# First-stage pieces, degree operations and clearing in other slots of a four-layer graph kernel

## The reference

```python
x = layernorm(x + L0(x, adj))            # prelu(adj @ (x @ W) + bias)
x = layernorm(x + L1(x, adj))            # adj @ (x @ weight) + bias
x = layernorm(x + L2(x, adj, nodemask))  # 5 rounds of message passing with a gated cell:
    # A = (adj != 0); m = h @ weight[l]; agg = A.T @ m
    # r, z = sigmoid(...); n = tanh(i_n + r * h_n); h = (1 - z) * n + z * h
x = layernorm(x + L3(x, adj, ...))       # 5 groups of the first 25 nodes: two graph convolutions each,
    # norm_adj = dinv * (adj + I) * dinv, dinv = deg ** -0.5, mixed with softmax(fusion_w)
```

## Time and profile before

| | us |
|---|---|
| median of 3 runs | 990.35 (988.59 to 992.75) |
| profiled execution | 988.7 |
| its span, first to last instruction | 986.9 |
| PE busy | 950.6 (96%) |
| DVE busy | 820.8 (83%) |
| ACT busy | 770.9 (78%) |
| POOL busy | 749.0 (76%) |

### The profile page before, as it was taken

How to read it: one execution, slowest core, us unless ns; L and a number is a source line. 1 busy time by engine, 2 the same in 40 slices (tenths; PEclk the granted TensorE clock), 3 DMA queues, 4 the chain that set the end, 5 groups by cost and what they waited for, 6 DMA issues and landing times.

```text
span 986.9 us, 19418 instructions
## 1 busy us (share of the span) xinstructions
PE 950.6 (96%) x6010; PEld 574.5 (58%) x6010; DVE 820.8 (83%) x2077; ACT 770.9 (78%) x1324; POOL 749.0 (76%) x844
## 2 busy tenths in 40 slices
PE   7999998999999999999999999999999999989894
PEld 6999996554444544444554555554445455468783
DVE  5999998898879999988898899789879987946555
ACT  5698896888887877887887889788887977865552
POOL 4777888567989897987988798889778887974101
PEclk9999999999999999999999999999999999999997
DMA  7543450333744563375448345654943563440020
GB/s 191 132 119 108 131 129 18 63 72 65 118 75 65 102 115 81 59 133 105 81 80 154 76 66 115 115 107 89 164 88 55 108 127 67 77 91 18 26 66 28
DMA packets 295406, 90.74 MB, mean 92 GB/s; under 512 B 222514, under 2 KB 295175, under 8 KB 295303
## 3 DMA queue, kind: packets, MB, share of 16 engines
q1 hardware_dynamic: 295302, 89.49, 45.8%
HBM read 28.67 MB, written 8.81 MB: 38 GB/s over the span
## 4 chain that ended last, share of the span: by engine, by line
PE 71%; DVE 10%; POOL 6%; issue 6%; ACT 3%; DMA 2%; SPq 0%; POOLq 0%; DVEq 0%; ACTq 0%
PE psum L1560 16%; PE psum L1565 16%; PE psum L1561 16%; PE psum L1485 8%; PE psum L1592 6%; POOL shared L765 2%; PE psum L1640 2%; PE psum L1673 2%; DMA shared<-shared 1%; DVE x3q L1020 1%; PE psum L1659 1%; PE psum L1483 1%; DVE shared L1342 1%; PE psum L1518 1%; DVE shared L1349 1%
## 5 line engine op out<-in xcount | busy, mean ns | idle before, releaser
L765 POOL TENSOR_TENSOR shared<-shared 128x512 f32<-128x512 f32 x160 | 203.7, 1273 | 34.6 <-ACT shared L974 34.5
L724 POOL TENSOR_TENSOR shared<-shared 128x512 f16<-128x512 f32 x128 | 148.3, 1158 | 52.9 <-ACT shared L928 52.8
L1565 PE MATMUL psum<-shared,wx_hi 128*128 128x512 f16 x480 | 182.1, 379 | 2.0 <-DVE shared L1368 1.7
L1560 PE MATMUL psum<-shared,wh_hi 128*128 128x512 f16 x480 | 182.2, 380 | 0.5 <-DVE shared L1342 0.4
L1560 PE MATMUL psum<-shared,wx_hi 128*128 128x512 f16 x480 | 181.9, 379 | 0.0
L1561 PE MATMUL psum<-shared,wx_lo 128*128 128x512 f16 x480 | 181.9, 379 | 0.0
L1565 PE MATMUL psum<-shared,wh_hi 128*128 128x512 f16 x480 | 181.9, 379 | 0.0
L1561 PE MATMUL psum<-shared,wh_lo 128*128 128x512 f16 x480 | 181.9, 379 | 0.0
L1342 DVE SCALAR_TENSOR_TENSOR shared<-psum,bhn,shared 128x512 f32<-128x512 f32 x160 | 119.9, 749 | 52.4 <-ACT shared L945 49.9
L974 ACT ACTIVATE shared<-psum,brz,unscale 128x512 f32<-128x512 f32 x160 | 124.2, 776 | 46.2 <-PE psum L1565 46.1
L910 ACT ACTIVATE shared<-psum 128x512 f16<-128x512 f32 x160 | 95.6, 597 | 52.7 <-PE psum L1592 52.7
(11 more groups left out here) (183 smaller groups left out, 1742.8 us busy)
## 6 DMA issues: line engine op xcount, KB each, us to landing
m<-in_adj_dram SPq DMA_DIRECT2D x32, 256.0 KB, 3.0
m<-in_x_dram SPq DMA_DIRECT2D x32, 256.0 KB, 3.4
adjr<-in_adj_dram SPq DMA_DIRECT2D x32, 256.0 KB, 3.2
out_dram<-x SPq DMA_DIRECT2D x8, 768.0 KB
shared<-shared SPq DMA_TRANSPOSE x192, 3.2
out_dram<-shared SPq DMA_DIRECT2D x32, 50.0 KB
v<-in_L_gnn_W_dram SPq DMA_DIRECT2D x10, 128.0 KB, 2.4
x3q<-x SPq DMA_DIRECT2D x16, 50.0 KB
```

What stands on the lines that cost most here:

```text
L724: nc.gpsimd.tensor_tensor(HT_LO[s % 2], HT[s][:, :], HT_HI[s % 2], ALU.subtract).then_inc(b_htl, 1)
L765: nc.gpsimd.tensor_tensor(ZH[s % 2][:, :], ZW[s % 2][:, :], HT[s][:, :], ALU.mult).then_inc(b_zh, 1)
L1560: mm(dst, w_h[:, col:col + P], h[:, :], start=start, stop=False)
L1565: return mm(dst, w_h[:, col:col + P], lo[:, :], start=False, stop=stop)
```

## The change

`piece_of` subtracts `FIRST_PIECE = 3`, so that each piece of the first stage stands three slots later (3 to 32 instead of 0 to 29). PE's inner products stand in slots 4 and 9, its outer products in 6, 11 and 16, POOL's scalings in 7, 12, 17 and 22. The degree operations of DVE get other slots in eight of 20 places, the seven powers of POOL stand in 24, 25, 26, 28, 29, 30 and 31, and the memset of slot 31, which could not wait there for the later end of the first stage, is gone from the head of the list, with one in slot 111 at its end.

```diff
         def piece_of(t):
+            t -= FIRST_PIECE
             if not 0 <= t < SLOTS_A:
                 return None
             k = ALONE + t // PIECES
...
-L3_AT = (3, 4, 8, 9, 13, 14, 32, 33, 44, 45, 46, 47, 48, 49, 52, 53, 64, 65, 66, 67)
-POW_AT = (15, 16, 17, 19, 27, 28, 30)
+L3_AT = (6, 7, 12, 16, 17, 22, 33, 43, 44, 45, 46, 47, 48, 49, 52, 53, 64, 65, 66, 67)
+POW_AT = (24, 25, 26, 28, 29, 30, 31)
 AN_AT = 70
 ZERO_PARTS = 8
-ZERO_AT = (31, 45, 46, 50, 51, 65, 66, 70, 71, 85, 86, 90, 91, 105, 106, 110)
+ZERO_AT = (45, 46, 50, 51, 65, 66, 70, 71, 85, 86, 90, 91, 105, 106, 110, 111)
+FIRST_PIECE = 3
```

## The result

The median went from 989.84 us (22 runs, 986.10 to 992.75) to 993.15 us (22 runs, 990.76 to 999.13): a ratio of 1.0035, interval 1.0024 to 1.0046. The kernel became 3.3 us slower; 993.5 was forecast. The profiled execution took 992.25 us with a span of 990.5, 3.6 more than before. So small a difference has to be read from starts of the same instruction in the same slot, not from busy times.

What follows compares the result with a forecast made beforehand. PE was taken as the bound of the recurrence, so any delayed slot delays the end. Hand-over +0.5, powers +2.6, small terms +0.1 and 0 made +3.2 us on a median of 990.35: 993.5 us, range 988.5 to 998.

Steps and rivals of the forecast that it cites:

- The hand-over: First stage to recurrence, up to slot 4: 1.5 us gained against 2.0 of products moved behind; +0.5 us, +0.2 to +0.7.
- The guess on L687: POOL's last L687 of the first stage might take 1.04 instead of 1.52, making slot 4's gain 1.8 instead of 1.3.
- (b): Slot 4: PE waits from about 168.9 to 171.1 for stream 2's transposed x, issued behind POOL's first L748.
- (a): Slot 2: PE waits for DVE's L1368, which stands behind two L1323; about 1.1 us lost.
- Rival 1: Hand-over waits are hidden in later slack and POOL's queue has room; -2.7 us, 987.7, chance 0.12.
- The powers: Powers and scalings in slots 22 to 26 make POOL's L724 late, so PE waits on transposes; +2.6 us, 0 to 5.1.
- rival 2: Hand-over as forecast, but POOL absorbs the powers; +0.5 to +0.6 us, 991, chance 0.13.
- rival 3: Transpose behind the late L724 lands later than 3.7 us, PE waits 5.1; +5.7 us, 996, chance 0.11.
- POOL is level again: Behind slot 27, which has no power, POOL has caught up and the powers of slots 28 to 31 fit.
- rival 4: POOL's delay continues through slots 28 to 31, second wait at slots 32 to 34; +1 to +2 more, 995, chance 0.09.
- The degrees' run: DVE's degree operation moved from slot 33 to 43 makes a run of seven with those of 44 to 49; 0, +-0.4.
- The rule on the shared ports: DVE or POOL, first to issue, blocks the other; about 1 us for powers beside L1376 in slots 30, 31, left out.

Runs made afterwards that it cites:

- e4: Changed kernel with DVE's product of the powers (L1173) in slot 34 instead of 33; median 991.81 us, ratio 1.0025 against the kernel before.
- e7: Changed kernel with three powers moved from slots 24, 25, 26 to 18, 19, 20; median 992.60 us, ratio 1.0033 against the kernel before.
- e1: Changed kernel with degree operations and powers back in their old slots, pieces still three slots later; median 989.59 us, ratio 1.0002 against before.
- e3: Changed kernel with POOL's first L748 (state of stream 0) ahead of the first stage's last step; median 993.79 us, ratio 1.0034 against before.
- e6: e5 with DVE's two adjacency L1323 of slots 1 and 2 behind the work of slots 2 and 3; median 987.70 us, ratio 0.9980 against before.
- e2: Changed kernel with the pieces in their old slots, degree operations, powers and memsets as changed; median 994.00 us, ratio 1.0040 against before.
- e5: Changed kernel with the edits of e1 and e3 together; median 989.11 us, ratio 0.9998 against the kernel before.
- e8: e6 with the power of slot 17 moved to 18, away from POOL's scalings; median 986.92 us, ratio 0.9978 against the kernel before.
- e9: Changed kernel, its degree operations kept, with early first L748 and late adjacency L1323; median 991.10 us, ratio 1.0011 against the kernel before.
- e10: The kernel of e3 run once more, unchanged, for another profile; single time 995.83 us.
- e11: The kernel of e3 run again, unchanged, for a second further profile; single time 994.24 us.

## Why the prediction held, and where it didn't

**The hand-over: +0.5, measured +0.52 at slot 26.** That the numbers agree to 0.02 is luck: e4 and e7, which have the same hand-over, stand at +0.38 and +0.06 there, and e1 at -0.1 without its wait of slot 19. So it is -0.1 to +0.5, at the lower side of what was forecast. The first product stands at 159.73 (159.7), slot 3 is 2.39 earlier (2.45), slot 4 has its wait of 1.95 (about 2) and a product at 171.70 (171.3 to 171.8); the gain there is 1.37, between the two values of 1.3 and 1.8 and below the 1.5 taken. The guess on L687 was right (1.04); that it began 0.25 later took back half of it. That the two waits are what they were said to be is shown by e3 (the early L749 removes (b)) and e6 (the later adjacency removes (a)): with both gone slot 4 is 3.6 us earlier than in the changed kernel. Rival 1 falls by that: the gap's gain isn't there by itself.

**The powers: +2.6, measured +2.71 between slots 26 and 30.** The queue's sum ended at 285.8, the row at 286.73. Of this 0.9 half is PE's own new delay, which POOL's steps follow (the scalings begin at 262.47 instead of 261.93). The other half is the power inside the scalings of slot 22: 1.46 us instead of the 1.0 that lies in the 1.75 of the sum, because it began while DVE's L1377 (262.65, 0.68 us) was running; more on this below. e7 shows that three powers carry the whole term, which rules out rival 2. Of the transposes issued from 270 to 300 none took over 4.1 us to land, so rival 3 didn't come. e2 shows that the scalings of slot 22, which the moved pieces put there, make up about half of it: without them 1.27 is lost instead of 2.71.

**Missed: slot 33, +1.14.** Here a step failed: "Behind slot 27, which has no power, POOL is level again; the powers of 28 to 31 then fit". I had asked of these powers whether they make POOL's transposes late, but not who waits for their result. The move of the product itself, from slot 32 to 33, isn't named in the prediction at all. Before, the last power ended at 298.39, and DVE's L1172 came to it 0.2 us later; POOL had no power in slot 29. Now POOL has four powers and no idle time over 0.1 us from 289.73 on, the last power ends at 307.60, and DVE's L1173, in a queue where PE's operations stand behind it, comes to it at 306.0. So an operation of the degrees cost its wait, where the prediction had charged such an operation "at most its own length". e2 has it without the pieces and e4 takes it away. It is of rival 4's size and place, but not its mechanism, which was POOL's queue; that one is real too, as e7's slot 32 shows, only hidden in the changed kernel.

**The degrees' run: 0, measured +0.3 at slot 44**, inside the bound of 0.4. The memsets and loads: behind slot 85 PE has one wait over 0.4 us that the kernel before doesn't have, 0.62 on ACT's L946 in slot 123. Slots 119 and 121 are shorter by 0.8 together, so nothing of it is left at the end.

**The clock and the medians.** The median moved by +3.3 and the sum was +3.2, but the profile has +4.9 at slot 50: the missed 1.14, the 0.3 of slot 44 and small things are in it. That the median shows no more is in part the granted clock. Within each kernel, the runs with a mean granted clock of 0.992 or more are shorter than the rest, by 1.8 to 3.5 us at the median. Of the changed kernel 16 of 22 runs are of this kind, with a median of 992.79. Of the kernel before only the runs beside the experiments have their clock on record, on three chips: 42 of 86 are of this kind, with medians of 988.55, 988.78 and 988.79. Like against like the change costs 4.0 to 4.2, near the +4.55 of the profile at slot 161. The others in the same way, against their own chip (us, number of runs):

| e1 | e2 | e3 | e4 | e5 | e6 | e7 | e8 | e9 |
|---|---|---|---|---|---|---|---|---|
| +0.9 (10) | +3.1 (4) | +2.8 (5) | +2.9 (9) | -0.5 (7) | -1.4 (10) | +2.5 (6) | -2.9 (9) | +2.2 (11) |

So that the sum was met to 0.1 us is luck: a missed cost of about 1 us met medians that set more runs at the higher clock (the changed kernel) against fewer (the kernel before). Whether the change has a part in these shares or chance alone made them isn't shown. The forecast's direction and size stand either way.

**The rule on the shared ports.** The sum left out 1.1 us that it would have charged to the powers beside L1376. The changed kernel's rows of POOL and DVE's L1377 (L1376 before) in PE's slots 30 and 31:

```profile
296.10 1.63 POOL L707 TENSOR_TENSOR v<-v,half 128x8 f32<-128x8 f32 x1
296.28 0.68 DVE L1377 SCALAR_TENSOR_TENSOR shared<-x,shared 128x512 f16<-128x512 f32 x1
...
299.81 1.27 POOL L766 TENSOR_TENSOR shared<-shared 128x512 f32<-128x512 f32 x1
300.63 1.00 DVE L1377 SCALAR_TENSOR_TENSOR shared<-x,shared 128x512 f16<-128x512 f32 x1
...
301.04 2.08 POOL L707 TENSOR_TENSOR v<-v,half 128x8 f32<-128x8 f32 x1
```

A power that runs already doesn't hold up L1377: the one at 296.28 began inside it and took its usual 0.68. So what the earlier trace rows showed for L1323 holds for this operation too, and leaving the 1.1 out was right. The L1377 of 1.00 began beside the wide L766; in the kernel before one beside the same L765, with no power near, took 0.87 (293.05). The other way round there is a price that neither the sum nor the rule had put on the powers: a power that begins while L1377 is running takes 2.08 instead of 1.64. So it is in all eight profiles that have such a pair (the changed kernel, e2, e3, e4, e7, e9, e10 and e11: 2.08 or 2.09), and the power of four columns in the scalings takes 1.46 instead of 1.01. In PE's starts nothing of it is seen at once (slots 30 and 31 are 4.35 and 4.45 long), but from 301.04 POOL has no idle time until the last power ends. So about 0.4 of the 1.69 for which L1173 waits is this; that is an estimate from these rows. The rule of the Trainium skill, SBUF — State Buffer, Who interferes with whom, that the first to issue holds the other up for its whole instruction, thus agrees where DVE's or POOL's wide operation was first (0.2 to 0.4 us lost where they overlap by 0.3 to 0.6 in these rows), and disagrees where the power was first.

## What to carry over

When an operation is moved to a later slot, ask of it two things: what its engine's queue does late behind it, and which engine comes to its result, with what queued behind that wait; the second cost a third as much as all the rest here and was missed. Ask the same of an operation that moves along with it: the distance in slots between the last power and its product stayed at two, and it was the queue ahead of the power that had grown. A gap on the bounding engine closes only when every engine that feeds the next slots is free too: here one POOL operation and a pair of DVE's had to move with the products, and only kernels with both (e6, e8) and without the new places of the powers were faster than before. And a wait removed ahead of another in the same queue can uncover the second (e7), so judge a placing by the last slot that it touches. Last, before two medians some us apart are compared, look at the mean granted clock of their runs.

## What was not expected of the hardware

PE idle for 1.95 us in slot 2 was followed by some 3.4 us at 1.2 GHz in three of four profiled executions of kernels with the early L749 and the adjacency ahead (e5, e10, e11: the windows of 4 us at a granted clock of 0.57 to 0.60), and by none in the fourth (e3), with the same wait. It cost 1.7 us over slots 2 and 3 each time. In e6, e8 and e9, where PE isn't idle for over 0.6 us there, no such stretch came. In the changed kernel the same 1.95 us of idle time in slot 4 was followed by a clock of 1.00 throughout:

```profile
150.00:175.00 25.00, 21.32 (x152) 14.89 (x151) 20.84 (x70) 17.14 (x36) 21.67 (x29) 1.00 0.12 22
```

What tells the two apart isn't settled. Nor does this stretch by itself make the two groups of e3's runs: e5 has it in a run whose mean granted clock is 0.993, as in the lower group, and every kernel here, also those that aren't idle there, has runs at a lower mean clock that are some 2 to 3.5 us longer. What e10 and e11 have over e3 is this stretch, one near 880 and, in e10, a longer one near 920. How much of e3's median each of them makes isn't shown.
